# One activation table for logarithm and exponential, and the bids' sigmoid by way of the exponential, in a two-layer kernel on one core

## The chip, the cores and the metric

One core of a Trainium2 chip runs the whole program. The metric is the device time of one execution in microseconds (us): the median of three runs. The engines are named as in the profile: PE (TensorE, with PEld for its weight loads), DVE (VectorE), ACT (ScalarE), POOL (GpSimd) and SP (SyncE, which here issues DMA transfers).

## The reference

Input x is 4 x 2048 tokens of 256 channels, float32. Two layers follow each other; each has an "attention" part and an "ffn" part, with modulated layer norms in front and gated residuals behind. What matters here:

```python
# layer 0, attention: a state-space scan over the tokens
gate = silu(xn @ W_gate)
dt = clip(softplus(z @ W_dt + b_dt), 0.001, 1.0)
h  = exp(dt * A) * h + dt * B * z            # 16 states for each of 512 channels
y  = sum over states of h * C, times gate
# layer 0, ffn: a router's softmax over 8 experts, one expert, exact gelu
probs = softmax(x @ Wr.T);  y = (gelu(x @ W1 + b1) @ W2 + b2) * probs[:, 7]
# layer 1, attention: a second scan, with beta = sigmoid(x @ Wbeta + b_beta)
# layer 1, ffn
conf = sigmoid([h @ conf_rwkv, h @ conf_trans])        # 3 values a token
difficulty = sigmoid(h @ w_diff)                       # 1 value a token
bids = conf * capital_shares * difficulty + h @ W_aff
winner = argmax(bids);  scale = conf[winner] / (conf[winner] + 1e-6)
```

The winner's output (two experts with squared relu, one with a product of two projections) is scaled and added.

## The kernel before

The tokens are cut into 16 chunks of 512 (4 for each batch row). Every engine's program is written out as one list, by chunks. Its backbone is `S_STEPS`, 98 steps a chunk: 23 marks, then 68 units (16 states x 4 blocks of 128 channels, and four steps more for what trails), then the tail. Unit k of a chunk is: ACT fills PSUM bank A0 or A1 in turn with the decay exp(dt * a) (line 1288), DVE runs the scan over the 512 tokens from it and from the input `bu` that POOL has made (lines 1527 and 1100), PE turns the scanned block so that tokens lie on the partitions (line 1760), and DVE multiplies it with C and adds it into `acc` (line 1491). `bu` has 4 buffers; `bb`, the row of B spread over the partitions, has 2, each filled by a DMA for one state (line 930).

Beside the backbone run other streams: `n_stream` prepares a chunk's scan, `f_stream` is layer 0's ffn, `x_stream` is layer 1, `w_stream` the weights' preparation at the start. `weave` puts the pieces of each stream between the steps by due steps in the table `PACE`, one number for each piece and engine. Layer 1 of a chunk falls so into the scan stages of the two chunks after it. Each engine does its list strictly in order; waits are on semaphores, so a wait holds up all that stands behind it on that engine. The last chunk's pieces have due steps of their own (`last_`, `end_`).

The pieces that the change touches, in ACT's order within a chunk: `dt0..3` (Exp of the bias-added product, line 1250), `gate0..3` (Silu, 1256), `ct`, `z0..3`, `softplus0` (Ln of dt + 1, line 1273, due step 10), `softplus1` (16), `lexp` (the router's Exp, line 1329, due 119, which is step 21 of the chunk after), `softplus2` and `3` (21); the units from step 23 on; Tanh pieces `r0`, `r1` (line 1409, due 230 and 231, so steps 34 and 35 two chunks on) and `sW0`, `sW1` (line 1413); `gelu0`, `gelu1` (line 1342); `sg`, the sigmoid of the four values of the bids (line 1428, due 246, step 50). `sg` works on 4 values for each of 4 tokens a partition, 16 elements.

ACT evaluates its functions from a table. A load of a table (`ACT_TABLE_LOAD` in the profile) is placed by the builder ahead of an activation whose function the last loaded table doesn't hold; the kernel before names none itself.

On DVE the piece `choice` (lines 1690 to 1710) waits for `sg`, then makes the bids, the winner and the coefficients in 14 small steps. Each step is followed by a wait for its own semaphore (`own_step`), and `OWN["dve_x"]` states how many such signals `x_stream` gives in a chunk. POOL multiplies `z` by `dt` and then by the first state's row of B (lines 1141 and 1147) as soon as the softplus of a block is there.

Of the kernel before, what the change touches and what calls it, by code (L numbers as in the profile page):

```python
# [8 lines left out]
ALU = mybir.AluOpType  # L9
ACT = mybir.ActivationFunctionType  # L10
# [35 lines left out]

SLOTS = ["ffn_0", "ffn_1", "rv", "sw", "e0_0", "e0_1", "e1_0", "e1_1"]
NSLOT = len(SLOTS)
CREDIT = 1
HB = F // 2 // P  # L50
NHB = F // P
# [34 lines left out]
class Bank:  # L86
# [5 lines left out]
    def fills_before(self, chunk, use):  # L92
        if use in self.last:
            return NCH * len(self.uses) + self.last.index(use) + CREDIT
        return chunk * len(self.uses) + self.uses.index(use) + CREDIT

# [63 lines left out]
def since(eng, sig, chunk, k=0):  # L160

    if sig.at(chunk, k) > 0:
        eng.wait_ge(sig.sem, sig.at(chunk, k))
# [95 lines left out]
def build(nc, w, out):  # L259
    ctx = ExitStack()  # L260
    with ctx:
# [22 lines left out]
        def signal(name, n, first=0):  # L284
            return Signal(sem(name), n, first)
# [129 lines left out]

        w_split = nc.dram_tensor("w_split", (NSLOT, P, 2 * KC * HB * P), F32, kind="Internal").ap()
        mods = nc.dram_tensor("mods", (B, len(ROWS) * C), F32, kind="Internal").ap()
# [5 lines left out]
                for name, uses in BANK_USES.items()}  # L423
        bank_of = {use: bank[name] for name in BANK_USES for use in BANK_USES[name]}
        last_bank_of = {use: bank[name] for name in LAST_USES for use in LAST_USES[name]}

        def bank_at(chunk, use):
            return last_bank_of[use] if chunk == NCH - 1 and use in last_bank_of else bank_of[use]
# [8 lines left out]
        def fill(eng, chunk, use):  # L437

            b = bank_at(chunk, use)
            if b.fills_before(chunk, use) > CREDIT:  # L440
                eng.wait_ge(b.free, b.fills_before(chunk, use))
# [13 lines left out]
        def kp(ap):  # L455
            return ap.rearrange("(k p) m -> p k m", p=P)
# [53 lines left out]
        for X, tag, first in ((X_ALL, "", 0), (X_LAST, "_last", NCH - 1)):  # L510
# [19 lines left out]
            X.x_x5 = signal(f"x_x5{tag}", 1, first)  # L530
            X.o_dve = signal(f"o_dve_x{tag}", OWN["dve_x"], first)
        s_w_last = {name: signal(f"s_w_{name}_last", 16, NCH - 1) for name in ("rv", "sw")}


        o_pool_n = signal("o_pool_n", OWN["pool_n"])
        o_dve_f = signal("o_dve_f", OWN["dve_f"])

# [174 lines left out]
        with nc.Block() as block:  # L712

            @block.sync
            def _(sp):
                for semaphore in [x for b in bank.values() for x in (b.full, b.free)]:
                    sp.sem_inc(semaphore, CREDIT)
                for layer in range(2):
# [150 lines left out]
        def lane_of(j):  # L869

            return X_LAST if j == NCH - 1 else X_ALL
# [16 lines left out]
        def hidden_free(eng, j, name, k):  # L888

            if name == "c":  # L890
                if j == 0:
                    eng.wait_ge(v_low, NSLOT)
                elif j >= 2:
# [28 lines left out]
        with nc.Block() as block:  # L922

            @block.sync
            def _(sp):
# [132 lines left out]
                def w_stream(_):  # L1058
                    yield "fold"
                    for dst, src in ((w_s, w["L1_ffn_Ws"]), (w_2, w["L1_ffn_W2"])):  # L1060
                        sp.dma_start(dst[:, :, :], kp(src)).then_inc(u_fold, 16)
                    for n in range(NSLOT + 1):
                        if n < NSLOT:
                            yield f"in{n}"
# [20 lines left out]
            def _(pool):  # L1085
# [110 lines left out]
                def w_stream(_):  # L1196
                    for n in range(NSLOT):
                        yield f"low{n}"
                        pool.wait_ge(v_high, n + 1)
                        pool.tensor_tensor(wsp[n % 2][:, 1], wst[n % 2][:, :, :], wsp[n % 2][:, 0].bitcast(F32),  # L1200
                                           ALU.subtract).then_inc(v_low, 1)
# [4 lines left out]
            def _(act):  # L1206
# [6 lines left out]
                def n_stream(i):  # L1213
# [55 lines left out]
                           .then_inc(b.free, 1)  # L1269
                    for k in range(DB):  # L1270
                        yield f"softplus{k}"
                        act.wait_ge(s_clip.sem, s_clip.at(i, k + 1))
                        act.activation(dt[:, k, :], dt[:, k, :], ACT.Ln, bias=1.0).then_inc(s_dt.sem, 1)  # L1273

# [91 lines left out]
                def x_stream(j):  # L1366
                    X = lane_of(j)
                    yield "e_norm"
                    if j == 0:
                        for k in range(2):  # L1370
                            act.wait_ge(v_store[k], 16 * NSLOT // 2)
                    since(act, X.x_x5, j)
# [52 lines left out]
                    yield "sg"  # L1425
                    used(act, j, "bidsT")

                    act.activation(X.sg[:, :, :], X.bl[:, :, 0:4], ACT.Sigmoid).then_inc(X.x_sg.sem, 1)
                    for name in "op":
                        for k in range(NHB):  # L1430
                            use = f"{name}{k}"
# [7 lines left out]
                def w_stream(_):  # L1439
# [4 lines left out]
                    for n in range(NSLOT):  # L1444
# [10 lines left out]
                        act.activation(wsp[n % 2][:, 0], wst[n % 2][:, :, :], ACT.Copy).then_inc(v_high, 1)  # L1455

                weave(PACE["act"], step, n_stream, f_stream, x_stream, w_stream)

            @block.vector
            def _(dve):  # L1460
# [126 lines left out]
                def x_stream(j):  # L1587
                    X = lane_of(j)
                    own = Own(dve, X.o_dve, j)
                    own_step = own.step  # L1590
# [91 lines left out]
                    for k in range(KC):  # L1682
# [5 lines left out]
                                                 op0=ALU.add, op1=ALU.mult).then_inc(b.free, 1)  # L1688
                    yield "choice"
                    dve.wait_ge(X.x_sg.sem, X.x_sg.at(j, 1))  # L1690
                    own_step(dve.tensor_tensor(X.bid[:, :, :], X.sg[:, :, 0:3], cs_row[:, :].unsqueeze(1)
                                               .to_broadcast([P, NT, 3]), ALU.mult))
                    own_step(dve.tensor_tensor(X.bid[:, :, :], X.bid[:, :, :], X.sg[:, :, 3:4].to_broadcast([P, NT, 3]),
# [44 lines left out]
                def w_stream(_):  # L1738
# [14 lines left out]
                    dve.memset(carrier[:, :], 0.0).then_inc(v_late, 1)  # L1753

                weave(PACE["dve"], step, n_stream, f_stream, x_stream, w_stream)

            @block.tensor
# [260 lines left out]
                weave(PACE["pe"], step, n_stream, f_stream, x_stream, w_stream)  # L2018


OWN = {"pool_n": 5, "dve_f": 8, "dve_x": 51}


# [20 lines left out]
```

## Time and profile before

| | |
|---|---|
| median of 3 runs | 3285.47 us (3280.89 to 3286.68) |
| span of the profiled execution | 3287.9 us |
| busy: PE, DVE, ACT, POOL | 88%, 83%, 64%, 59% |
| instructions | 45422 |

"Busy" is the time in which an engine has an instruction running; waits, branches and DMA issues aren't counted. In the timelines a row is one instruction or a run of like ones (x3); its first number is the start in us from the span's start, its second the time from the start of the first to the end of the last, and "idle before" names what ended the wait in front of it. Rows of one engine overlap a little, since the end of an instruction and the start of the next do. "issue" as the reason of a wait means that the profile shows nothing that the engine waited for.

### The profile page before, as it was taken

The numbers are of one execution on the slowest core, as the hardware profiler recorded it, in microseconds if no ns is written. First come the engines' busy times: TensorE is split into PE (matmuls) and PEld (weight loads), VectorE is DVE, ScalarE is ACT, GpSimd is POOL, SyncE is SP. The second block draws the span as 40 slices with busy tenths as digits, with TensorE's granted clock in tenths as the row PEclk, the third lists the DMA queues.
The fourth block names the chain that finished last, engine by engine and source line by source line (L and its number), as shares of the span: only waits on it lengthen the run. The fifth ranks groups of instructions, "written<-read, shape, count | busy, mean of one in ns | idle before, by whom it ended". The sixth has DMA issues, their size and how long they took to land.

```text
span 3287.9 us, 45422 instructions
## 1 busy us (share of the span) xinstructions
PE 2907.9 (88%) x14848; PEld 2380.8 (72%) x14848; DVE 2739.3 (83%) x4612; ACT 2096.2 (64%) x3852; POOL 1925.7 (59%) x1541
## 2 busy tenths in 40 slices
PE   6567698998999899898989989899999989998898
PEld 4455477787877778687777868777777877777676
DVE  3777989797998979799898979889897989989541
ACT  2546476676757677675767767576766767575433
POOL 1766667564766757475675756576575647666110
PEclk8558699999999999999999999999999999999998
DMA  4241123231322323232322323232232323223122
GB/s 130 96 159 39 52 81 111 92 102 64 129 82 91 125 78 100 70 118 85 100 103 81 106 79 125 66 106 92 87 109 86 108 76 121 78 71 120 56 103 76
DMA packets 152778, 308.56 MB, mean 94 GB/s; under 512 B 18368, under 2 KB 96984, under 8 KB 135136
## 3 DMA queue, kind: packets, MB, share of 16 engines
q1 hardware_dynamic: 152000, 302.52, 27.6%
q8 instruction: 119, 1.95, 0.2%
q10 hardware_dynamic: 272, 1.57, 0.1%
q0 software_dynamic: 272, 1.57, 0.1%
q14 instruction: 115, 0.94, 0.1%
HBM read 288.27 MB, written 17.35 MB: 93 GB/s over the span
## 4 chain that ended last, share of the span: by engine, by line
PE 48%; DVE 18%; issue 13%; ACT 12%; POOL 5%; DMA 1%; DVEq 0%; SPq 0%; POOLq 0%; ACTq 0%
PE ps_B L1870 11%; PE ps_B L1765 10%; PE ps_A L1765 8%; DVE hs L1527 8%; PE ps_H L1760 7%; DVE acc L1491 5%; PE ps_H L1778 4%; PE ps_B L1760 3%; POOL bu L1100 3%; PE ps_B L1778 3%; PE ps_B L1917 2%; ACT ps_A L1288 2%; DMA bb<-b_rows 1%; DVE hA L1719 1%; ACT acc L1300 1%
## 5 line engine op out<-in xcount | busy, mean ns | idle before, releaser
L1100 POOL TENSOR_TENSOR bu<-z,bb 128x512 f32<-128x512 f32 x1024 | 1294.2, 1290 | 289.9 <-DVE hs L1527 146.7
L1527 DVE TENSOR_TENSOR_SCAN hs<-ps_A,state,bu 128x512 f32<-128x512 f32 x768 | 976.5, 1276 | 21.7 <-ACT ps_A L1288 11.4
L1288 ACT ACTIVATE ps_A<-dt,a_neg 128x512 f32<-128x512 f32 x1024 | 699.3, 686 | 355.7 <-DVE hs L1527 351.5
L1760 PE MATMUL ps_H<-ident,hs 128*128 128x128 f32 x4096 | 652.6, 294 | 195.3 <-DVE acc L1491 123.1
L1760 PEld LDWEIGHTS ps_H<-ident,hs 128*128 128x128 f32 x4096 | 528.3, 151 | 329.2 <-DVE acc L1491 152.0
L1870 PE MATMUL ps_B<-ws_out,hid 128*128 128x256 f32 x2944 | 699.4, 382 | 15.5 <-ACT hid L1437 6.1
L1491 DVE SCALAR_TENSOR_TENSOR acc<-ps_H,ctok,acc 128x512 f32<-128x512 f32 x960 | 700.2, 731 | 8.0 <-PE ps_H L1760 7.1
L1870 PEld LDWEIGHTS ps_B<-ws_out,hid 128*128 128x128 f32 x2944 | 537.0, 191 | 85.1 <-ACT hid L1437 9.9
L1765 PE MATMUL ps_B<-fh,ws_in 128*128 128x512 f32 x1440 | 537.6, 418 | 10.3 <-DVE bl L1680 4.3
L1527 DVE TENSOR_TENSOR_SCAN hs<-ps_A,bu 128x512 f32<-128x512 f32 x256 | 310.9, 1216 | 32.2 <-ACT ps_A L1288 20.0
L1765 PEld LDWEIGHTS ps_B<-fh,ws_in 128*128 128x128 f32 x1440 | 271.0, 188 | 70.5 <-DVE cb L1664 8.1
L1765 PE MATMUL ps_B<-fl,ws_in 128*128 128x512 f32 x720 | 281.9, 391 | 0.0
L1435 ACT ACTIVATE hid<-ps_B 128x512 f32<-128x512 f32 x256 | 149.9, 586 | 174.0 <-PE ps_B L1765 173.4
L1765 PE MATMUL ps_B<-f1h,ws_in 128*128 128x512 f32 x512 | 180.4, 409 | 58.7 <-ACT hid L1334 24.1
L1141 POOL TENSOR_TENSOR z<-z,dt 128x512 f32<-128x512 f32 x64 | 87.0, 1360 | 161.6 <-ACT dt L1273 161.0
L1765 PEld LDWEIGHTS ps_B<-f1h,ws_in 128*128 128x128 f32 x512 | 96.7, 189 | 98.2 <-ACT hid L1334 36.9
L1437 ACT ACTIVATE hid<-hid 128x512 f32<-128x512 f32 x256 | 161.6, 631 | 8.1
L1091 POOL TENSOR_TENSOR rs_f<-rs_f,mhalf 128x4 f32<-128x4 f32 x16 | 16.3, 1017 | 251.9 <-DVE rs_f L1471 251.9
L1595 DVE TENSOR_TENSOR fl<-ff,fh 128x512 fp32r<-128x512 f32 x60 | 46.3, 792 | 134.3 <-ACT fh L1364 134.3
L1765 PEld LDWEIGHTS ps_B<-fl,ws_in 128*128 128x128 f32 x720 | 136.5, 190 | 19.1
L1091 POOL TENSOR_TENSOR rs_x<-rs_x,mhalf 128x4 f32<-128x4 f32 x45 | 49.6, 1103 | 160.9 <-DVE rs_x L1471 160.9
L1778 PE MATMUL ps_H<-w_out,yT 128*128 128x256 f32 x512 | 118.3, 385 | 3.7 <-issue 1.2
(349 smaller groups left out, 4807.7 us busy)
## 6 DMA issues: line engine op xcount, KB each, us to landing
ws_in<-w_split SPq DMA_DIRECT2D x126, 1024.0 KB, 5.4
bb<-b_rows SPq DMA_DIRECT2D x256, 256.0 KB, 3.9
ws_out<-in_L_ffn_V_rwkv SPq DMA_DIRECT2D x64, 512.0 KB, 5.8
ws_out<-in_L_ffn_W SPq DMA_DIRECT2D x32, 512.0 KB, 6.9
xb<-in_L_attn_x SPq DMA_DIRECT2D x16, 512.0 KB, 5.3
n<-in_L_attn_x SPq DMA_DIRECT2D x16, 512.0 KB, 3.9
w_split<-wsp SPq DMA_DIRECT2D x8, 1024.0 KB, 5.6
out<-xb SPq DMA_DIRECT2D x16, 512.0 KB, 3.2
```

The source lines that it names most:

```text
L1091: pool.tensor_tensor(rs[:, :], rs[:, :], mhalf[:, :], ALU.pow).then_inc(own_sig.sem, 1)
L1100: pool.tensor_tensor(bu[:, u % 4, :], z[:, d, :], bb[:, s % 2, :], ALU.mult)\
L1141: pool.tensor_tensor(z[:, k, :], z[:, k, :], dt[:, k, :], ALU.mult).then_inc(s_u.sem, 1)
L1288: act.activation(b.t[:, :], dt[:, d, :], ACT.Exp, scale=a_neg[:, d, s:s + 1])\
L1435: act.activation(hid[:, k, :], b.t[:, :], ACT.Relu).then_inc(b.free, 1)
L1437: act.activation(hid[:, k, :], hid[:, k, :], ACT.Square).then_inc(X.x_sq.sem, 1)
L1491: dve.scalar_tensor_tensor(out=acc[:, t, :], in0=b.t[:, :], scalar=ctok[:, t, s:s + 1], in1=acc[:, t, :], op0=ALU.mult, op1=ALU.add).then_ ...
L1527: dve.tensor_tensor_scan(hs[:, s % 2, d, :], b.t[:, :], bu[:, k % 4, :], state[:, s, d:d + 1] if i % CPB else 0.0, ALU.mult, ALU.add)\
L1760: return pe.transpose(dst, src, ident[:, :])
L1765: last = pe.matmul(dst, a, b, start=n == 0, stop=n == len(prods) - 1)
L1778: last = pe.matmul(b.t[:, t % 2 * C:(t % 2 + 1) * C], act[:, k, t * P:(t + 1) * P], wt[:, k, :], start=k == 0, stop=k == kb - 1)
L1870: last = pe.matmul(b.t[:, t % 2 * C:(t % 2 + 1) * C], hid[:, k, t * P:(t + 1) * P], wt[:, k % HB, :], start=k == 0 and t % 2 == 0, stop=k ...
```

## The change

It is made of two parts. Ahead of the first softplus of each chunk (`softplus0`) a table load is written by hand, with the number of the table that holds both the logarithm and the exponential (`EXP_LN`). And the sigmoid of the bids becomes exp(-x) on ACT in the same place, with two steps on DVE at the head of `choice`: plus one, then the reciprocal, in place in `sg`. `OWN["dve_x"]` goes from 51 to 53.

```diff
@@ -46,6 +46,8 @@
 
 SLOTS = ["ffn_0", "ffn_1", "rv", "sw", "e0_0", "e0_1", "e1_0", "e1_1"]
 NSLOT = len(SLOTS)
+
+EXP_LN = 6
 CREDIT = 1
 HB = F // 2 // P
 NHB = F // P
@@ -424,6 +426,10 @@
         bank_of = {use: bank[name] for name in BANK_USES for use in BANK_USES[name]}
         last_bank_of = {use: bank[name] for name in LAST_USES for use in LAST_USES[name]}
 
+        def table_of_exp_and_ln(act):
+            act.add_instruction(mybir.InstLoadActFuncSet(name=nc.get_next_instruction_name(), engine=act.engine,
+                                                         act_func_set_id=EXP_LN))
+
         def bank_at(chunk, use):
             return last_bank_of[use] if chunk == NCH - 1 and use in last_bank_of else bank_of[use]
 
@@ -1269,6 +1275,8 @@
                            .then_inc(b.free, 1)
                     for k in range(DB):
                         yield f"softplus{k}"
+                        if k == 0:
+                            table_of_exp_and_ln(act)
                         act.wait_ge(s_clip.sem, s_clip.at(i, k + 1))
                         act.activation(dt[:, k, :], dt[:, k, :], ACT.Ln, bias=1.0).then_inc(s_dt.sem, 1)
 
@@ -1425,7 +1433,7 @@
                     yield "sg"
                     used(act, j, "bidsT")
 
-                    act.activation(X.sg[:, :, :], X.bl[:, :, 0:4], ACT.Sigmoid).then_inc(X.x_sg.sem, 1)
+                    act.activation(X.sg[:, :, :], X.bl[:, :, 0:4], ACT.Exp, scale=-1.0).then_inc(X.x_sg.sem, 1)
                     for name in "op":
                         for k in range(NHB):
                             use = f"{name}{k}"
@@ -1688,6 +1696,8 @@
                                                  op0=ALU.add, op1=ALU.mult).then_inc(b.free, 1)
                     yield "choice"
                     dve.wait_ge(X.x_sg.sem, X.x_sg.at(j, 1))
+                    own_step(dve.tensor_scalar(X.sg[:, :, :], X.sg[:, :, :], 1.0, None, ALU.add))
+                    own_step(dve.reciprocal(X.sg[:, :, :], X.sg[:, :, :]))
                     own_step(dve.tensor_tensor(X.bid[:, :, :], X.sg[:, :, 0:3], cs_row[:, :].unsqueeze(1)
                                                .to_broadcast([P, NT, 3]), ALU.mult))
                     own_step(dve.tensor_tensor(X.bid[:, :, :], X.bid[:, :, :], X.sg[:, :, 3:4].to_broadcast([P, NT, 3]),
@@ -2018,7 +2028,7 @@
                 weave(PACE["pe"], step, n_stream, f_stream, x_stream, w_stream)
 
 
-OWN = {"pool_n": 5, "dve_f": 8, "dve_x": 51}
+OWN = {"pool_n": 5, "dve_f": 8, "dve_x": 53}
 
 
 # ---- launch: one core; inputs and outputs as the reference has them ----
```

## Rows read from the trace of the kernel before

**Rows 1.** The page: span, and busy time of each engine
```profile
span 3287.9 us, 45422 instructions
...
PE 2907.9 (88%) x14848; PEld 2380.8 (72%) x14848; DVE 2739.3 (83%) x4612; ACT 2096.2 (64%) x3852; POOL 1925.7 (59%) x1541
```

**Rows 2.** Window, chunk 6: from:to, length, busy us of PE, PEld, DVE, ACT, POOL
```profile
1257.60:1326.40 68.80, 66.86 (x366) 56.69 (x364) 68.44 (x82) 48.99 (x102) 53.88 (x46) 1.00 0.34 113
```

**Rows 3.** Timeline of ACT, chunk 6, from the softplus to the scans
```profile
1192.56 1.28 ACT L1273 ACT_TABLE_LOAD   x1
...
1198.90 1.28 ACT L1329 ACT_TABLE_LOAD   x1
1200.19 0.23 ACT L1329 ACTIVATE lg<-lg 128x32 f32<-128x32 f32 x1
```

**Rows 4.** Timeline of DVE, chunk 6, the same stretch
```profile
1198.35 0.84 DVE L1563 TENSOR_TENSOR lg<-lg,lg_m 128x32 f32<-128x32 f32 x1
...
1201.67 0.68 DVE L1595 TENSOR_TENSOR fl<-ff,fh 128x512 fp32r<-128x512 f32 x1
1202.27 3.62 DVE L1527 TENSOR_TENSOR_SCAN hs<-ps_A,state,bu 128x512 f32<-128x512 f32 x3
1206.15 6.26 DVE L1527 TENSOR_TENSOR_SCAN hs<-ps_A,state,bu 128x512 f32<-128x512 f32 x5 [0.26 <-POOL bu L1100]
1212.63 1.28 DVE L1527 TENSOR_TENSOR_SCAN hs<-ps_A,state,bu 128x512 f32<-128x512 f32 x1 [0.21 <-issue]
```

**Rows 5.** Timeline of POOL, chunk 6, the same stretch
```profile
1194.62 1.28 POOL L1141 TENSOR_TENSOR z<-z,dt 128x512 f32<-128x512 f32 x1 [8.06 <-ACT dt L1273]
...
1201.80 1.70 POOL L1100 TENSOR_TENSOR bu<-z,bb 128x512 f32<-128x512 f32 x1
...
1204.83 11.24 POOL L1100 TENSOR_TENSOR bu<-z,bb 128x512 f32<-128x512 f32 x9
```

**Rows 6.** Waits: who waited for what, us in total, times, longest
```profile
DVE hs L1527 <- POOL bu L1100: 13.0, 25, 1.6
```

**Rows 7.** Groups of ACT's instructions: busy us and mean ns, idle before
```profile
L1288 ACT ACT_TABLE_LOAD x30 | 38.5, 1283 | 0.6
...
L1329 ACT ACT_TABLE_LOAD x15 | 19.2, 1283 | 0.3
L1428 ACT ACT_TABLE_LOAD x15 | 19.2, 1283 | 0.3
```

**Rows 8.** Timeline of ACT, chunk 6, around the first Tanh
```profile
1214.87 0.59 ACT L1409 ACTIVATE cb<-ps_B 128x512 f32<-128x512 f32 x1
1215.78 0.69 ACT L1288 ACTIVATE ps_A<-dt,a_neg 128x512 f32<-128x512 f32 x1 [0.32 <-DVE hs L1527]
...
1218.72 0.60 ACT L1409 ACTIVATE cb<-ps_B 128x512 f32<-128x512 f32 x1 [1.64 <-PE ps_B L1765]
```

**Rows 9.** Timeline of PE, chunk 6, start of the second product (r1)
```profile
1217.05 0.48 PE L1765 MATMUL ps_B<-fh,ws_in 128*128 128x512 f32 x1
```

**Rows 10.** Timeline of DVE, chunk 6, the scan that takes that decay
```profile
1218.73 1.27 DVE L1527 TENSOR_TENSOR_SCAN hs<-ps_A,state,bu 128x512 f32<-128x512 f32 x1
```

**Rows 11.** Timeline of ACT, chunk 6, around the sigmoid
```profile
1250.89 1.28 ACT L1428 ACT_TABLE_LOAD   x1
...
1260.12 0.60 ACT L1435 ACTIVATE hid<-ps_B 128x512 f32<-128x512 f32 x1 [5.71 <-PE ps_B L1765]
```

**Rows 12.** Timeline of DVE, chunk 6, inside the choice
```profile
1254.82 0.17 DVE L1691 TENSOR_TENSOR bid<-sg,cs_row 128x12 f32<-128x12 f32 x1
...
1257.05 0.18 DVE L1707 RECIPROCAL wcs<-wcs 128x4 f32<-128x4 f32 x1
1257.26 0.16 DVE L1708 TENSOR_TENSOR wcs<-wcs,bmax 128x4 f32<-128x4 f32 x1
```

**Rows 13.** Timeline of DVE, tail of the run, behind the last choice
```profile
3227.64 0.88 DVE L1719 SCALAR_TENSOR_TENSOR hA_last<-ps_A,coef_last,hA_last 128x256 f32<-128x256 f32 x2 [1.28 <-PE ps_A L1778]
```

**Rows 14.** Timeline of DVE, chunk 5, second scan behind the choice
```profile
1073.08 1.28 DVE L1527 TENSOR_TENSOR_SCAN hs<-ps_A,state,bu 128x512 f32<-128x512 f32 x1 [0.51 <-issue]
```

## The prediction

> **What bounds the kernel now.** The page comes first [rows 1]: one core, span 3287.9 us, PE busy 88%, DVE 83%, ACT 64%. No engine is idle enough to be ignored, and none is full, so the shares decide nothing; the kernel has 16 chunks of about 189 us and has to be read by stage. I took chunk 6 (1192 to 1391 us) and checked its readings in the others.
>
> Second, the windows: in the scan stage DVE is busy 68.44 of 68.80 us [rows 2]. That stage is 64 scans and their read-outs in a fixed order, and DVE has no gap in it: a microsecond added to DVE there is added to the chunk, unless DVE next waits for something that did not move.
>
> Third, the start of the scan stage, on three engines. ACT loads a table at 1192.56, runs the first softplus, and after the last softplus loads another table at 1198.90 for the router's exponential [rows 3]. DVE starts scans 0 to 2 at 1202.27, then waits 0.26 us for POOL; scans 3 to 7 start 1.25 us apart; scan 8 waits 0.21 us more [rows 4]. POOL makes the scan inputs `bu`: it starts at 1194.62, when the first softplus is there, and from then on has no gap: `z`, `bu`, `z`, `bu`, ..., then nine `bu` in 11.24 us, 1.25 us each [rows 5]. Scan 3 starts 0.04 us after its `bu` ends (1204.83 + 1.25 = 1206.08, to within the rounding of merged rows). So the scan stage is started by POOL, POOL by the first softplus, and the second table load is not in that line. Over the run DVE's scans wait 13.0 us for `bu`, in 25 places [rows 6]; chunks 2 to 15 all have the wait before scan 3, 0.25 to 0.46 us long, and chunks 0 and 1 a longer one.
>
> **The change, part by part.** All prices are from one profiled execution (span 3287.9); the median of the runs is 3285.47, 2.4 us less and inside the runs' own spread of 5.8, so I work out a difference and add it to the median.
>
> *The load before the first softplus.* It takes the place of the one at 1192.56 [rows 3], one in each of 16 chunks. Same time, same place: 0.
>
> *The load before the router's exponential* (15 times 1.28 us [rows 7]) goes; in chunk 0, where the softplus is followed by the first decay, one of line 1288's 30 goes. The exponential needs DVE's subtraction, which ends at 1198.35 + 0.84 = 1199.19 [rows 4], so it can start at about 1199.24 instead of 1200.19 [rows 3]: 0.95 us earlier, not 1.28. Behind it come DVE's `prob`, one split, and scans 0 to 2, all 0.95 earlier. Scan 3 isn't: it waits for POOL, and what is late next is `bu`, every time until scan 7. Cover: POOL's queue. Worth 0 here. Bounds: if DVE and POOL get in each other's way differently (POOL's `bu` at 1201.80 took 1.70 instead of 1.27 while DVE's split ran [rows 4, 5]) scans 3 to 7 may move by 0.43 either way; the split still falls on one POOL instruction, the one before, so I take 0. Scan 8's 0.21 has no releaser in the trace; it may go since PE and ACT are ahead: between 0 and 15 x 0.21 = 3.2 us gained. I take 0, as the row calls it issue.
>
> *A table for Tanh.* Today the table loaded for the exponential at 1198.90 also serves the Tanh at 1214.87, for no load stands between. No row shows whether the new common table holds Tanh. If not, a load comes 14 times before line 1409 (chunks 2 to 15; the first two have no Tanh there), after which the decays' Exp needs none, as now. ACT's load then costs between 0 and 1.28 us. I take that it comes. What it delays: the Tanh from 1214.87 to 1216.15, and behind it in ACT's queue the decay at 1215.78, to about 1216.75 to 1217.4. ACT's next Tanh waits for PE until 1218.72, with 1.64 us idle before it [rows 8]. The decay is for the scan at 1218.73 [rows 10] (the scans take turns on two banks), 1.3 us later. PE's product `r1`, which starts at 1217.05 [rows 9], needs the bank that the Tanh frees, at 1216.75 instead of 1215.46: 0.3 us in hand. Cost 0; if the weight load ahead of `r1` wants the bank earlier, up to 14 x 0.2 = 2.8 us; if nothing covered it, 14 x 1.28 = 18 us.
>
> The Trainium skill, "ScalarE: Activation LUTs", section "Table sets: the hidden batching unit", names tanh among the functions in exp's set and only exp and ln for the common set. By that the load does come, as taken here; no row of this kernel shows it.
>
> *The bids' sigmoid.* Sigmoid's load (15) goes, and the Exp load behind it (line 1288; 14 of the 30 are this one, the others are those after Gelu and chunk 0's) [rows 7]. The last Sigmoid but one, in the tail, keeps a load, since Gelu's came before it. That is 2.57 us less on ACT in chunks 2 to 15, in chunk 6 from 1250.89 on. What waits for it? One decay, whose scan comes only behind DVE's choice, and after that ACT is idle 5.71 us for PE [rows 11]. DVE itself came for the sigmoid at 1254.82 [rows 12]. So 0: ACT idles longer. The new Exp activation costs what the Sigmoid did.
>
> In all ACT has 30 loads fewer (2 in each of 14 chunks, 1 in chunks 0 and 1): 30 x 1.28 = 38.5 us less of its 2096.2 [rows 1], none of it on the path by the above.
>
> The same page's section "What ACT_TABLE_LOAD costs" puts a switch at about 2.66 us, 1283 ns of load and 1380 of drain. By that ACT would be spared 80 us. Here the instruction starts 0.01 us behind the load (1198.90 + 1.28, 1200.19 [rows 3]), so the trace bears out the load and not the drain.
>
> *Plus one and reciprocal on DVE.* The 14 steps that are there, each waited for before the next, start 0.20 us apart in the mean (1254.82 to 1257.05 for eleven), the reciprocal 0.21 [rows 12]. The new two work on 16 elements a partition instead of 4: 2 x 0.21 = 0.42 us a chunk. They can't start early: DVE gets to them when it has done the two `tw` products. They lie before scan 26, in the stage without gaps. Choices 0 to 13 lie there: 14 x 0.42 = 5.9 us. Choice 14 and 15 lie in the tail; behind the last, DVE waits 1.28 us for PE [rows 13], so they cost 0.
> What takes some of it back: two scans later, in some chunks, DVE waits for `bu`, since POOL waits for a row of `b` whose transfer is queued behind weights. In chunk 5 this is 0.51 us [rows 14]; I find such waits in six of the 14 chunks, 0.2 to 0.7 us long (0.26, 0.51, 0.28, 0.69, 0.20, 0.42), which take back 0.26 + 0.42 + 0.28 + 0.42 + 0.20 + 0.42 = 2.0 us. In chunk 6 the `bu` is there 0.5 us early and nothing is taken back.
>
> **Sum.** 5.9 - 2.0 = +3.9 us: 3291.8 in the profile's terms, 3289.4 as median. Own range: with scan 8's gap gained 0.7; with nothing taken back and `r1` late 5.9 + 2.8 = 8.7. About 3286 to 3294.
>
> **Rivals.**
> 1. The start of the scan stage does follow ACT: the 0.95 us passes through, because POOL too gains from DVE being out of its way earlier. 15 x 0.95 = 14.3 us gained, 5.9 lost: 3277.1. For it: ACT has no gap between softplus, load and exponential [rows 3], and DVE is behind it. Against: `bu` ends just before each of scans 3 to 7.
> 2. Slower: the Tanh load is on the path. It decides if PE's `r1` or the decay behind it has less in hand than 1.28 us; by the rows they have 1.6 and 2.3. Price up to 14 x 1.28 = 18: 3285.5 + 3.9 + 17.9 = 3307.3.
> 3. The hand-written load isn't counted by what places the others: then the softplus has two loads, 1.28 us on the line softplus, POOL, scan in 16 chunks, and the exponential's loads stay: 3285.5 + 20.5 + 3.9 = 3309.9.
>
> The skill's rule in the same page, "Rules for kernel authors", to group by table set and to use the common set for exp and ln, would have the time fall, as rival 1 does. The trace agrees that the loads fall away, and not that anybody waits for them.
>
> **How the numbers follow.** Forecast 0.70, rival 1 0.12, rival 2 0.12, rival 3 0.06. The forecast is the likeliest: 3289.4. The medians themselves are uncertain by some 3 us (the runs spread over 5.8), so the forecast's range becomes 3282 to 3296. For 8 in 10 part of the rivals, which may come in at a fraction, is taken in: 3279 to 3298. A change under 0.2% (6.6 us) can't be told from none here. Faster than 3278.9 is rival 1 at nearly full price, 0.12; slower than 3292.0 is rivals 2 and 3 and the upper end of the forecast's own range, 0.25; between them 0.63.
>
> **What would show it.** Right: 80 loads instead of 110; scan 3 still 0.03 us behind its `bu` and 12.3 us behind the first softplus, with its wait grown from 0.26 to about 1.2 us; 16 steps at the choice, 0.42 us more; the wait of chunk 5 down from 0.51 to 0.1; ACT's idle time up by what it is spared. Wrong: scan 3 earlier after the softplus (rival 1); PE idle before `r1` for ACT, or scans waiting for a decay (rival 2); two loads in a row before the softplus (rival 3). What would also make it wrong is a new order of DVE and POOL on their shared work, 0.4 us a time, which the trace of before can't tell.

## The result: 3294.03 us, and the profile of the changed kernel

| | before | changed |
|---|---|---|
| median of 16 runs each | 3285.66 (3280.89 to 3287.78) | 3294.03 (3284.95 to 3299.27) |
| span of the profiled execution | 3287.88 | 3297.48 |
| ratio of the times, 95% interval | | 1.0018 (1.0010 to 1.0026) |

By the ratio, 0.18%, that is under the prediction's bound of 0.2% and on the slow side of none. By the medians it is over it: they are 8.4 us apart, 0.26%, and 3294.03 lies above the prediction's 3292.0, in the stretch to which it gave 0.25. The median is 4.6 us above the forecast and inside the range. The two measures part where times lie in two groups, as the changed kernel's do: six of 16 at 3285.0 to 3287.4, ten at 3293.8 to 3299.3; the profile is of the upper one. In one other kernel such a gap lies in TensorE's clock in the tail, as is shown further down; no profile caught the lower group of this one.

The page of the changed kernel (its parts are those of [rows 1]), then the groups of ACT's table loads ([rows 7]) and the wait of DVE's scans for POOL ([rows 6]):

```profile
span 3297.5 us, 45424 instructions
...
PE 2920.5 (89%) x14848; PEld 2379.6 (72%) x14848; DVE 2745.5 (83%) x4644; ACT 2059.5 (62%) x3822; POOL 1929.1 (59%) x1541
```

```profile
L430 ACT ACT_TABLE_LOAD x16 | 20.5, 1283 | 0.3
...
L1296 ACT ACT_TABLE_LOAD x15 | 19.2, 1283 | 0.3
L1417 ACT ACT_TABLE_LOAD x14 | 18.0, 1283 | 0.2
```

```profile
DVE hs L1535 <- POOL bu L1106: 48.3, 40, 16.9
```

ACT has 30 instructions and 36.7 us fewer: the loads are 80 instead of 110 (with 16 each for Silu and Gelu, one in the tail and two at the start). L430 is the load by hand, L1296 the decays' after Gelu, L1417 the one that comes ahead of Tanh. DVE has 32 instructions more. And DVE waits 48.3 us for `bu`, where it waited 13.0: 16.9 us of it is one wait in the first chunk that the profile of before put down to ACT (17.6), and the other 18.4 us more are new, 14 times 1.26 in chunks 2 to 15 and 0.7 in chunk 0: what ACT gave up at the router stands again as DVE's wait for POOL.

The start of the scan stage in chunk 6, timelines of ACT, DVE and POOL, to be laid beside [rows 3 to 5]:

```profile
1192.96 1.28 ACT L430 ACT_TABLE_LOAD   x1
1194.26 0.63 ACT L1281 ACTIVATE dt<-dt 128x512 f32<-128x512 f32 x1
...
1199.62 0.23 ACT L1337 ACTIVATE lg<-lg 128x32 f32<-128x32 f32 x1 [0.32 <-DVE lg L1571]
```

```profile
1200.84 0.68 DVE L1603 TENSOR_TENSOR fl<-ff,fh 128x512 fp32r<-128x512 f32 x1
1201.44 2.45 DVE L1535 TENSOR_TENSOR_SCAN hs<-ps_A,state,bu 128x512 f32<-128x512 f32 x2
1204.08 1.28 DVE L1535 TENSOR_TENSOR_SCAN hs<-ps_A,state,bu 128x512 f32<-128x512 f32 x1 [0.19 <-POOL bu L1106]
1206.69 6.26 DVE L1535 TENSOR_TENSOR_SCAN hs<-ps_A,state,bu 128x512 f32<-128x512 f32 x5 [1.33 <-POOL bu L1106]
1213.16 1.28 DVE L1535 TENSOR_TENSOR_SCAN hs<-ps_A,state,bu 128x512 f32<-128x512 f32 x1 [0.21 <-issue]
```

```profile
1195.03 1.28 POOL L1147 TENSOR_TENSOR z<-z,dt 128x512 f32<-128x512 f32 x1 [8.09 <-ACT dt L1281]
...
1200.86 1.82 POOL L1147 TENSOR_TENSOR z<-z,dt 128x512 f32<-128x512 f32 x1
...
1205.38 9.97 POOL L1106 TENSOR_TENSOR bu<-z,bb 128x512 f32<-128x512 f32 x8
```

From the first softplus (1194.26) to scan 0 it is 7.18 us instead of 8.42, but to scan 3 it is 12.43 instead of 12.30. All of chunks 2 to 15 show it (12.41 to 12.45, before 12.28 to 12.32); chunks 0 and 1 are within 0.03 us of what they were. POOL's eight products up to that scan's take 11.60 us instead of 11.46. The row to see is POOL's `z` at 1200.86: 1.82 us, where this instruction otherwise takes 1.28. DVE's `prob`, its split `fl` and the first scan ran beside it. Before, DVE's split and scan fell on the `bu` at 1201.80 and stretched it to 1.70 [rows 5].

The choice in the same chunk, timeline of DVE:

```profile
1255.35 0.17 DVE L1699 TENSOR_SCALAR sg<-sg 128x16 f32<-128x16 f32 x1
1255.55 0.25 DVE L1700 RECIPROCAL sg<-sg 128x16 f32<-128x16 f32 x1
1255.83 0.17 DVE L1701 TENSOR_TENSOR bid<-sg,cs_row 128x12 f32<-128x12 f32 x1
```

The two new steps take 0.20 and 0.28 us, 0.48 together, from start to start.

To find where the rest lies I cut the run at the starts of certain rows (first softplus, scans 3, 8, 26, 28 and 63 of a chunk) and added each stretch up over chunks 2 to 15, all from one profile per kernel. "Front" is from a chunk's last scan to the next chunk's first softplus (13 of them), "start" what lies before chunk 2's first softplus, "tail" from the last scan of all. Last column: us of the middle (chunks 2 to 15) in which PE was granted 1.2 GHz, not 2.4. In us:

| kernel | start | softplus to scan 3 | scans 3 to 8 | 8 to 26 (choice) | 26 to 28 | 28 to 63 | fronts | tail | span | at 1.2 GHz |
|---|---|---|---|---|---|---|---|---|---|---|
| before | 437.0 | 172.2 | 90.5 | 629.2 | 76.1 | 1027.1 | 608.2 | 247.7 | 3287.9 | 115.5 |
| changed | 436.4 | 174.1 | 90.4 | 635.7 | 73.7 | 1027.8 | 608.3 | 251.0 | 3297.5 | 122.8 |
| changed, third profile | 433.6 | 174.1 | 90.4 | 635.5 | 73.2 | 1027.7 | 606.4 | 249.7 | 3290.5 | 117.3 |
| table alone | 433.1 | 174.1 | 90.4 | 629.4 | 75.1 | 1027.1 | 606.6 | 250.7 | 3286.5 | 116.2 |
| sigmoid alone | 436.6 | 172.2 | 90.5 | 635.6 | 73.1 | 1028.8 | 608.1 | 250.1 | 3295.0 | 120.5 |
| two more steps | 436.4 | 174.1 | 90.7 | 641.9 | 73.0 | 1028.5 | 609.5 | 250.7 | 3304.9 | 130.0 |
| router's load back | 435.5 | 172.2 | 90.8 | 635.5 | 73.2 | 1028.1 | 607.3 | 247.4 | 3289.9 | 119.3 |
| another load, then Tanh's | 434.4 | 174.2 | 90.4 | 645.9 | 73.2 | 1027.7 | 610.4 | 250.3 | 3306.5 | 126.8 |

The scan stages (the five columns in the middle) went from 1995.0 to 2001.8 us, +6.8; in the third profile of the changed kernel it is +5.8. That part is the steadier one from profile to profile. Start, fronts and tail together are not steady: +2.8 in the first profile, -3.2 in the third. The tail alone is 2.0 to 3.3 us longer in both: the clock record has PE at 1.2 GHz for 13.7 us from some 30 us behind the last scan on, where it is 10.2 us in the kernel before.

### The profile page after: what moved, and what is told of

It reads as the page before. It is cut to its first block, busy times and chain, and to the rows that moved or that the text cites. A ratio compares the mean times of both kernels' runs of the same rounds, so it can differ in the third digit from the quotient of the medians.

```text
span 3297.5 us, 45424 instructions
## 1 busy us (share of the span) xinstructions
PE 2920.5 (89%) x14848; PEld 2379.6 (72%) x14848; DVE 2745.5 (83%) x4644; ACT 2059.5 (62%) x3822; POOL 1929.1 (59%) x1541
## 4 chain that ended last, share of the span: by engine, by line
PE 47%; DVE 17%; issue 13%; ACT 10%; POOL 7%; DMA 3%; SPq 0%; DVEq 0%; POOLq 0%; ACTq 0%
PE ps_B L1775 10%; PE ps_B L1880 10%; DVE hs L1535 8%; PE ps_A L1775 8%; PE ps_H L1770 7%; DVE acc L1499 5%; POOL bu L1106 4%; PE ps_H L1788 4%; DMA bb<-b_rows 3%; PE ps_B L1770 3%; PE ps_B L1927 2%; PE ps_B L1788 2%; POOL z L1147 2%; DVE hA L1729 1%; ACT ps_A L1296 1%
## 5 line engine op out<-in xcount | busy, mean ns | idle before, releaser
L1296 ACT ACTIVATE ps_A<-dt,a_neg 128x512 f32<-128x512 f32 x1024 | 699.2, 686 | 381.7 <-DVE hs L1535 377.8
L1880 PEld LDWEIGHTS ps_B<-ws_out,hid 128*128 128x128 f32 x2944 | 536.2, 191 | 90.8 <-issue 14.1
L1147 POOL TENSOR_TENSOR z<-z,dt 128x512 f32<-128x512 f32 x64 | 94.8, 1482 | 160.9 <-ACT dt L1281 160.1
L1603 DVE TENSOR_TENSOR fl<-ff,fh 128x512 fp32r<-128x512 f32 x60 | 46.2, 790 | 136.6 <-ACT fh L1372 136.6
```

What stands on the lines that cost most here:

```text
L1147: pool.tensor_tensor(z[:, k, :], z[:, k, :], dt[:, k, :], ALU.mult).then_inc(s_u.sem, 1)
L1296: act.activation(b.t[:, :], dt[:, d, :], ACT.Exp, scale=a_neg[:, d, s:s + 1])\
L1880: last = pe.matmul(b.t[:, t % 2 * C:(t % 2 + 1) * C], hid[:, k, t * P:(t + 1) * P], wt[:, k % HB, :], start=k == 0 and t % 2 == 0, stop=k ...
```

## The experiments

The edits are shown shortened: slices, semaphore updates, the definitions of the numbers of tables and the count `OWN` are left out.

**One part at a time.** `e1_table_only` keeps the Sigmoid activation and leaves the two DVE steps out; `e2_sigmoid_only` leaves the tables to the builder.

```diff
 e1, against the changed kernel
-  act.activation(X.sg, X.bl[:, :, 0:4], ACT.Exp, scale=-1.0)
+  act.activation(X.sg, X.bl[:, :, 0:4], ACT.Sigmoid)
-  own_step(dve.tensor_scalar(X.sg, X.sg, 1.0, None, ALU.add))
-  own_step(dve.reciprocal(X.sg, X.sg))
 e2, against the changed kernel
-  if k == 0:
-      table_of_exp_and_ln(act)
```

> The hand-written table load ahead of softplus0 alone; the bids keep their Sigmoid and DVE its 14 steps. Theory (the time is lost at DVE's two new steps, 0.48 us in each of 14 chunks, and the loads are hidden): the router's load is gone as in the changed kernel, and scans 3 to 7 start 12.43 us after softplus0 instead of 12.29, since POOL's z product at 1200.86 is stretched by DVE's split to 1.82 us: +0.14 us in 14 chunks, 2 us in all; s8 to s26 as before. Median about 2 us over the kernel before. Rival (the Tanh load or the new table is what costs): it carries the whole loss, 6 to 8 us. Rival 1 of the prediction (a removed load at the start is on the path): 10 us or more faster.

> The bids' sigmoid as Exp on ACT plus two steps on DVE; no table load by hand, so softplus keeps its own and the router's Exp its load; Sigmoid's load and the one behind it go. Theory: choice 0.48 us longer in 14 chunks, 6.7 us, of which about 2 are taken back where DVE waited for bu two scans later: 4 to 5 us over the kernel before; scan 3 at 12.29 us after softplus0 as before. Rival (the table costs): within 1 us of the kernel before.

Measured: the table alone 3288.3 us against 3286.51 of before (ratio 1.0003, 0.9995 to 1.0012), the sigmoid alone 3292.93 (1.0015, 1.0006 to 1.0023). In the table above the two effects stand apart, each in its own column: 14 x 0.14 = 2.0 us from softplus to scan 3 with the table alone, 14 x 0.46 = 6.4 at the choice with the sigmoid alone, 2.9 of it taken back two scans later. In the scan stages 1.2 and 5.3 make 6.5, against 6.8 for both; the medians' 1.8 and 6.4 make 8.2, against 8.3 for the changed kernel on the same chip. So the hand-loaded table, which takes away the 15 loads ahead of the router's exponential, gains nothing. By the stages it costs 1 to 2 us; the times alone do not show that, since their interval holds 1.

**The choice has no cover.** `e4_two_more_steps` adds two steps of the same size, and `after_again` is the changed kernel once more, on the same chip.

```diff
   own_step(dve.reciprocal(X.sg, X.sg))
+  own_step(dve.tensor_scalar(X.sg, X.sg, 1.0, None, ALU.mult))
+  own_step(dve.tensor_scalar(X.sg, X.sg, 1.0, None, ALU.mult))
```

> The changed kernel with two further steps (times one, on 16 elements a partition) behind the reciprocal: the suspected cost doubled. Theory: each step starts 0.20 us after the one before, 0.40 us a chunk, 5.7 us over the changed kernel less what waits for bu are left to take back (under 0.5): about 5 us over it, 11 over the kernel before. Rival (DVE has slack at the choice): 0.

> The changed kernel once more, for a second profile. Its 16 runs fell into two groups, 3285 to 3287 and 3294 to 3299 us, at a mean granted clock of 0.941 to 0.943 and 0.937 to 0.940. Theory: what differs between the groups is how long PE's clock stays at the lower level where PE has been idle, in the chunks' fronts and above all in the tail (247.7 us from the last scan in the kernel before, 251.0 in the changed kernel's profile, with nothing else changed there); DVE's stages are equal to 0.1 us a chunk. Rival: the groups differ in the scan stage (waits for bu).

Measured: 3305.53 us (ratio 1.0053, 1.0038 to 1.0068), 10.7 above the 3294.85 of the changed kernel beside it, where about 5 were expected. The stage with the choice grew by 6.2 (14 x 0.44), and nothing more was taken back, so the mechanism holds and the sum doesn't. Against the profile of `after_again` (span 3294.2; choice 635.9, start 433.8, fronts 608.1, tail 250.3, 120.2 us at 1.2 GHz) the span is 10.7 longer: 6.1 at the choice, 2.6 at the start, 1.4 in the fronts, 0.4 each in the tail and from scan 3 to 8. The steps themselves are the 6.1. The 1.4 in the fronts go with 3.6 us more at 1.2 GHz there. The 2.6 at the start do not go with the clock (239 us at 1.2 GHz there, against 242); that column differs by as much between profiles of the changed kernel itself, and why is left open.

**The router's load back.** `e5_router_load_back` puts a load by hand ahead of the router's exponential.

```diff
+  table_of_exp_and_ln(act)
   act.activation(lg, lg, ACT.Exp)      # lexp
```

> The changed kernel with a table load of 1.28 us put back ahead of the router's Exp. Theory (a load there is hidden behind POOL, and without it DVE's split falls on POOL's z product, 1.82 us, instead of on bu, 1.70): scans 0 to 2 start later again, but scan 3 comes 12.29 instead of 12.43 us after softplus0, 2 us over 14 chunks, so this kernel is about 2 us faster than the changed one although it does more. Rival (the load's removal is worth something): 5 us or more slower.

Timelines of ACT, DVE and POOL of this kernel, chunk 6:

```profile
1199.08 1.28 ACT L430 ACT_TABLE_LOAD   x1 [0.32 <-DVE lg L1572]
1200.38 0.23 ACT L1338 ACTIVATE lg<-lg 128x32 f32<-128x32 f32 x1
```

```profile
1202.14 3.62 DVE L1536 TENSOR_TENSOR_SCAN hs<-ps_A,state,bu 128x512 f32<-128x512 f32 x3
1206.03 6.29 DVE L1536 TENSOR_TENSOR_SCAN hs<-ps_A,state,bu 128x512 f32<-128x512 f32 x5 [0.27 <-POOL bu L1106]
```

```profile
1200.32 1.27 POOL L1147 TENSOR_TENSOR z<-z,dt 128x512 f32<-128x512 f32 x1
1201.68 1.70 POOL L1106 TENSOR_TENSOR bu<-z,bb 128x512 f32<-128x512 f32 x1
```

The load is there, 1.28 us on ACT in each chunk, and the stretch from softplus to scan 3 is *shorter* by 1.9 us over the run (172.2, as before): DVE comes later, POOL's `z` stays at 1.27, and the next `bu` takes 1.70. The wait of scan 3 is back to 0.27. The median was 3293.78, the changed kernel's own; its ten executions (3290.6 to 3297.2) cannot show 1.9 us.

**The bids' two loads back.** `e6_bid_loads_back` puts a load by hand ahead of the bids' Exp and one behind it.

```diff
+  table(act, EXP_ONLY)
   act.activation(X.sg, X.bl[:, :, 0:4], ACT.Exp, scale=-1.0)
+  table(act, EXP_ONLY)
```

> The changed kernel with two table loads put back around the bids' Exp, 2.57 us of ACT a chunk. Theory (ACT idles 5.7 us behind them): all stages as in the changed kernel, to 1 us over 14 chunks. Rival (the freed ACT time is used by somebody): 5 us or more slower.

Timeline of ACT, chunk 6:

```profile
1250.46 1.28 ACT L434 ACT_TABLE_LOAD   x1 [1.02 <-DVE bl L1694]
1251.76 0.22 ACT L1441 ACTIVATE sg<-bl 128x16 f32<-128x16 f32 x1
1251.99 1.28 ACT L434 ACT_TABLE_LOAD   x1
...
1258.69 0.60 ACT L1449 ACTIVATE hid<-ps_B 128x512 f32<-128x512 f32 x1 [4.72 <-PE ps_B L1781]
```

3294.9 us, and the five columns of the scan stages are within 0.7 us of the changed kernel's. The 32 loads cost nothing here: ACT still idles 4.72 us for PE behind them.

**What is in hand ahead of Tanh.** The forecast had 1.6 us in hand for the Tanh load. A first try, `e3_two_tanh_loads`, wrote a twin load there.

```diff
+  table(act, EXP_ONLY)      # e3
+  table(act, EXP_ONLY)
   act.activation(X.cb[:, k, :], b.t[:, :], ACT.Tanh, scale=0.5)     # r0
```

> The changed kernel with one more table load of 1.28 us ahead of the first Tanh (two instead of one) in 14 chunks. Theory: the first load is covered, with about 0.2 us in hand before PE's product r1 (bank free at 1217.41, r1 at 1217.59 in the changed kernel's chunk 6), so the second isn't: r1 starts about 1.1 us later and DVE's second cb step waits for it, 0.5 to 1.1 us a chunk, 7 to 15 us in all over the changed kernel, in the stage from scan 8 to scan 26. If ACT has a slack of more than 2.6 us there: that stage is as in the changed kernel, 635.7 us over 14 chunks.

```profile
L434 ACT ACT_TABLE_LOAD x14 | 18.0, 1283 | 0.2
```

The group of loads has 14 at that line, not 28. Of the two loads of one table a single one remains, so this was the changed kernel again (3294.63 us), and it says nothing of the slack. The second try loads another table first.

```diff
+  table(act, SIGMOID)       # e10
+  table(act, EXP_ONLY)
```

> The changed kernel with a load of another table (Sigmoid's) and then of Tanh's, both ahead of the first Tanh of the stage, so that the Tanh comes another 1.28 us later in 14 chunks. The twin loads of one table tried for this before did not both remain in the trace. The forecast had 0.3 us in hand at PE's product r1 behind the first load, and rows of the changed kernel show r1 0.54 us later than before in chunk 6 with no scan late. Theory (ACT's and PE's queues have slack there of over two loads against the scans): 94 loads instead of 80, r1 up to 1.28 us later, the sums of the scan stage unchanged, time within 3 us of the changed kernel (3291 to 3298). Rival (a load there is paid for once its slack is used up): scan 8 to 26 of each chunk up to 14 x 0.9 to 1.28 = 13 to 18 us longer, with scans waiting for a decay: 3306 to 3313.

Timelines of ACT, PE and DVE, chunk 6, behind the two loads; then ACT and PE of the changed kernel at the same place:

```profile
1217.29 2.57 ACT L435 ACT_TABLE_LOAD   x2
1219.87 0.60 ACT L1425 ACTIVATE cb<-ps_B 128x512 f32<-128x512 f32 x1
```

```profile
1220.52 0.50 PE L1783 MATMUL ps_B<-fh,ws_in 128*128 128x512 f32 x1 [0.91 <-ACT cb L1425]
```

```profile
1223.57 0.69 DVE L1680 SCALAR_TENSOR_TENSOR cb<-cb,ps_B 128x512 f32<-128x512 f32 x1 [0.47 <-PE ps_B L1783]
```

```profile
1215.52 1.28 ACT L1417 ACT_TABLE_LOAD   x1
1216.81 0.60 ACT L1417 ACTIVATE cb<-ps_B 128x512 f32<-128x512 f32 x1
...
1219.27 0.60 ACT L1417 ACTIVATE cb<-ps_B 128x512 f32<-128x512 f32 x1 [0.67 <-PE ps_B L1775]
```

```profile
1217.59 0.48 PE L1775 MATMUL ps_B<-fh,ws_in 128*128 128x512 f32 x1
```

The theory of much slack falls, and the rival holds. With one load PE's `r1` starts without a wait; with two it waits 0.91 us, DVE's product behind it 0.47, and the stage grows by 10.2 us, 0.73 a chunk. The time was 3309.07 (ratio 1.0068, 1.0053 to 1.0083), 15.7 above the changed kernel's 3293.36 on the same chip. Between the two profiles the span differs by 16.0: 10.4 in this stage, 4.0 in the fronts, 1.4 at start and tail. So of the second 1.28 us 0.55 were hidden: the first load fits with about half a microsecond to spare.

**Where ACT's line begins.** By the chain softplus, POOL, scan, time is to be gained ahead of the first softplus. `e8_load_early_sigmoid` is the kernel before with the common table loaded ahead of `z1`, in an idle 0.69 us of ACT. `e9_softplus_early` does that and runs softplus 0 and 1 ahead of `z2` and `z3` (due steps 6 instead of 10 and 16). `e11_softplus_early_no_table` is that order without the hand-loaded table.

```diff
 e9, against the kernel before
-  for k in range(DB): z{k}
-  for k in range(DB): softplus{k}
+  z0, table_of_exp_and_ln, z1, softplus0, softplus1, z2, z3, softplus2, softplus3
 e8: the load alone, in the same place; e11: the same order, no load
```

> The hand-written table alone (the bids keep their Sigmoid, DVE has no new steps), its load moved ahead of z1, where ACT waits for PE, and the first two softplus moved ahead of z2. If POOL's queue, started by the first softplus, sets the start of the scans, this must move it: POOL starts z and bu some 3 to 4 us earlier, and scan 3 then follows DVE's own work (scans 0 to 2 without a wait), about 1.5 us a chunk earlier than in the changed kernel: 20 us faster than it, 12 to 20 us faster than the kernel before. Rival (ACT's or PE's own work sets the start): within 5 us of the kernel before.

> The kernel before with the common table loaded by hand ahead of z1, where ACT is idle 0.69 us for PE, instead of right ahead of the first softplus; the bids' Sigmoid and the order of the steps kept. Theory (the line softplus, POOL, scan carries what ACT saves ahead of the softplus): the softplus comes 0.6 to 0.7 us earlier, 14 x 0.65 = 9 us gained, less the 2 us that the common table alone cost: 3278 to 3282. Rival (the start of the stage hangs on something else): 3287 to 3289.

> The kernel before with nothing but the order changed: softplus 0 and 1 ahead of z2 and z3; the tables are left to the builder, so the router's exponential has its load again. The same kernel with the common table took 3261.3. Theory (the load ahead of the router's exponential is worth nothing as long as POOL's queue covers it, and something as soon as it doesn't): with the softplus early POOL has its first four products done by 1182.8 and scan 3 waits only 0.24 us for bu, so the load's 1.28 us less 0.24 comes onto the path: first softplus to scan 3 some 14 x 1.0 = 14 us longer than with the common table, 3272 to 3278. Rival 1 (the common table is worth nothing here too, all of the 26 us are the order's): 3260 to 3264. Rival 2 (the order is worth nothing, the earlier place of the load was all of it): 3284 to 3287.

| kernel | median us | ratio, 95% | start | softplus to scan 3 | fronts | tail | span | at 1.2 GHz |
|---|---|---|---|---|---|---|---|---|
| e8 | 3283.0 | 0.9985 (0.9976 to 0.9995) | 429.1 | 184.2 | 598.5 | 241.0 | 3273.7 | 119.2 |
| e9 | 3261.32 | 0.9920 (0.9906 to 0.9935) | 425.6 | 211.5 | 553.0 | 247.7 | 3260.2 | 95.1 |
| e11 | 3307.45 | 1.0065 (1.0050 to 1.0080) | 426.8 | 242.4 | 566.2 | 250.1 | 3305.3 | 137.2 |

`e9` beats both kernels: it is 0.8%, 26 us, below the kernel before. Its span is 27.7 us shorter: 55.2 are gained in the fronts, of which 39.3 are given back from softplus to scan 3, and 11.4 are gained at the start. `e8` gained 9.7 us in the fronts, as expected, and gave 12.0 back from softplus to scan 3. The row that says why is POOL's second `z`, idle for a softplus that stands in ACT's queue behind a piece that waits for PE:

```profile
1189.86 1.28 POOL L1147 TENSOR_TENSOR z<-z,dt 128x512 f32<-128x512 f32 x1 [1.11 <-ACT dt L1281]
```

An earlier softplus 0 without an earlier softplus 1 is worth nothing in the middle of the run. What `e8` has left, 4.0 us between the medians (3278 to 3282 was expected, 3283.0 came), can be from the start, 8.0 us less in the profile, where profiles of the changed kernel differ by 2.9. The tail's 6.7 us less are those of the quickest of its executions, which is the one profiled, and not of the median.

`e11` missed what each theory had said. Timelines of ACT, DVE and PE, chunk 6, and a window over PE's 14 matrix products and transposes behind the norm (columns as in [rows 2]; the third number from the end is the granted clock):

```profile
1186.47 1.28 ACT L1274 ACT_TABLE_LOAD   x1
...
1199.07 1.28 ACT L1330 ACT_TABLE_LOAD   x1
```

```profile
1200.63 0.19 DVE L1568 TENSOR_REDUCE lg_m<-lg 128x4 f32<-128x32 f32 x1 [1.86 <-ACT lg L1330]
```

```profile
1190.94 1.97 PE L1761 MATMUL ps_B<-ident,nn 128*128 128x128 f32 x8 [2.40 <-ACT nn L1209]
```

```profile
1190.94:1195.06 4.12, 4.03 (x14) 3.26 (x14) 0.00 (x0) 1.09 (x2) 2.90 (x3) 0.60 0.00 0
```

The same in `e9`:

```profile
1174.80 1.28 ACT L430 ACT_TABLE_LOAD   x1
```

```profile
1186.57 0.19 DVE L1576 TENSOR_REDUCE lg_m<-lg 128x4 f32<-128x32 f32 x1 [0.44 <-ACT lg L1338]
```

```profile
1179.84 1.09 PE L1769 MATMUL ps_B<-ident,nn 128*128 128x128 f32 x8 [1.36 <-ACT nn L1215]
```

```profile
1179.84:1182.42 2.58, 2.49 (x14) 1.88 (x14) 0.00 (x0) 1.09 (x2) 2.50 (x3) 1.00 0.00 0
```

The spans of `e11` and `e9` differ by 45.1 us, nearly all of it three things. First, the fronts, 13.3 longer. The builder's load stands behind `z1`, right ahead of the softplus, where nothing hides it: from `z0` to the softplus it is 3.39 us instead of 2.59, 10.3 in 13 fronts. The other 2.9 lie ahead of `z0`; the fronts have 7.5 us more at 1.2 GHz. Second, the router's load is now on the path, since with the softplus early POOL is no longer the last: in five chunks scan 3 comes 1.26 us later after the softplus, nearly the whole load. Third, in the other nine it comes 2.6 to 2.9 later. There PE, which waits 2.4 us for the norm instead of 1.36, does the same 14 instructions in 4.12 us at a mean clock of 0.60 instead of 2.58 at 1.00, and its result is what the router waits for. The second and third make the 31.0 us from softplus to scan 3. (In the five chunks PE's wait was 2.40 us too, and the clock 1.00, so the wait alone doesn't decide the clock.)

So the common table is worth nothing to the order of the kernel before, and with its place ahead of `z1` up to 45 us to another order. No run has the early order with the common table loaded right ahead of the softplus, so table and place are told apart by these rows alone.

**A profile of the lower group.** `after_third` repeats the changed kernel.

> The changed kernel once more, for a profile of one of its quicker executions, since its times lie in two groups, 3284.7 to 3287.4 and 3293.8 to 3299.3. If this profile is of the lower group: the scan stages' sums as in the first profile (choice stage +6.5), and 8 to 10 us less between the last scan of a chunk and the next softplus or in the tail, where PE is at the lower clock less long. If it is of the upper group: as in the first profile, and the question stays open.

It had 3293.36 us (3284.84 to 3295.73), and its profile (3290.5) is again not of the lower group. What such a group is, the profile of `e8` shows by chance: its ten times are 3275.5, 3276.3 and eight from 3281.5 to 3284.8, and the profile is of the quickest. Window of 23.9 us over the tail, from 164 us after the last scan on in `e8` and then from 166 us on in the changed kernel of `after_again`, from where PE's clock falls in each:

```profile
3196.80:3220.70 23.90, 17.26 (x68) 13.03 (x69) 6.79 (x23) 7.92 (x14) 0.00 (x0) 0.79 0.27 104
```

```profile
3210.50:3234.40 23.90, 15.25 (x40) 10.73 (x41) 6.13 (x29) 5.47 (x10) 1.22 (x2) 0.50 0.35 132
```

In every other profile PE has 1.2 GHz for 23.9 us here; in that one it came back to full clock after 10.2 us, ran 68 products in the window instead of 40, and the tail took 241.0 us instead of 247.4 to 251.0. `e5`, with the same clock in the rest of its tail, has 247.4, so the stretch is worth 6.4 us; `e8`'s two quickest times lie 5 to 9 us below the others. That the changed kernel's lower group, 6 to 14 us below the upper, is the same is argued from this, not shown.

## Why the prediction was right, and where a term was off

The time is inside the stated range, and the path that the prediction told for each part is the one that the runs show. Its bound of 3292.0 for "slower" was passed, with 0.25 given to that.

*The load before the softplus, 0:* right. L430 has 16 rows of 1.28 us in the place of the old ones.

*The router's load, worth 0:* right that it isn't gained, with the mechanism as told: scan 0 comes 1.24 us sooner (forecast 0.95; `prob` is shorter too, 0.61 us where it was 0.86) and DVE waits 1.33 us before scan 3 (forecast about 1.2) and 0.19 before scan 2. The term was mis-sized by 2 us: it is +0.14 a chunk, not 0. The bound of 0.43 for "DVE and POOL get in each other's way differently" held it. I took 0, on the ground that the split would still fall on one POOL instruction. That ground was too weak: it does, but the instruction stretched is now `z`, with 1.82, instead of `bu`, with 1.70, and `e5` shows both cases with nothing else changed. Scan 8's gap of 0.21 stayed, as taken.

*The table for Tanh:* right. Fourteen loads at L1417. The Trainium skill, "ScalarE: Activation LUTs", section "Table sets: the hidden batching unit", names tanh beside exp, and for the common set only ln and exp, with the rest of its list left open; the 14 rows agree that a load comes. That the load costs nothing was right, but narrow: 0.3 us in hand at `r1` by the forecast, and `e10` shows that another 1.28 us costs 0.73 a chunk. Rival 2 was wrong about this load and right about the next.

*The sigmoid's loads, 0:* right, by `e6`. The drain of about 1380 ns that the Trainium skill, "ScalarE: Activation LUTs", section "What ACT_TABLE_LOAD costs", adds to a load is not seen: the softplus starts 0.02 us behind the load (1192.96 + 1.28, 1194.26), and ahead of all 16 loads of L430 ACT idles 0.3 us together.

*The two steps, 0.42 a chunk:* right place, a little small. They take 0.48: the reciprocal of 16 elements a partition runs 0.25 us (mean 253 ns of 15) and not 0.18 like that of 4. I had priced both by the pitch of steps on 4 to 12 elements. In the stage it comes to 6.5 us, 14 times 0.47, instead of 5.9.

*Taken back, 2.0:* 2.3 in the profile (26 to 28), 2.9 with the sigmoid alone. The wait of 0.51 in chunk 5 [rows 14] is gone altogether, not down to 0.1.

The sum for the scan stages was +3.9 and is +6.8 (5.8 in the third profile). By terms: +1.9 for the start of the stage, +0.6 for the steps, -0.3 for what is taken back, and +0.7 elsewhere in the scan stages, mostly from scan 28 to 63, whose cause is left open. The other 1.7 of the median's 4.6 us, and +2.8 of the profile, are start, fronts and tail, which the forecast did not carry as a term. The 1.7 is inside the 3 us that the prediction left to the medians; between the first and the third profile of the changed kernel these parts shrank by 6.0 (start 2.9, fronts 1.9, tail 1.3), and each of them has less time at 1.2 GHz in the third (242.3, 22.7 and 44.9 us against 249.2, 25.6 and 46.2).

*Rival 1*, that the stage's start follows ACT, is refuted by `e1` and `e5`; *rival 3*, two loads ahead of the softplus, by the count of L430. (Rival 1's price of 3277.1 leaves out the 2.0 us taken back; with them it is 3275.1. Nothing hangs on it.) The warning at the end, a new order of DVE and POOL, is what came.

## What to carry to other kernels

Before you price a removed stall, find the engine that is last at the next meeting point: here ACT gave up 36.7 us, and DVE waited for POOL instead. Then turn the question round: what would have to move so that the saving is on the path? Once two softplus steps ran earlier, the same table and its hand-picked place divided 3261 us from 3307. And count the instances of what an experiment inserted before reading its time: one of these was the unchanged program.

## What the runs showed of the hardware

Some elementwise instructions of POOL and DVE stretch where they meet, and most do not. POOL's 128x512 product goes from 1.28 us to between 1.66 and 1.82 only where it starts beside DVE's split `fl`: 27 products in the profile of before and 27 in that of the changed kernel, out of 28 such meetings in each (the other one takes 1.38). A split that starts when a product is well under way takes 1.15 us instead of 0.68 itself, and leaves that product at 1.28. Beside scans alone POOL's products keep 1.28 in the mean of some 950. DVE's subtraction of 128x32 takes 0.84 beside POOL's `z` [rows 4] and 0.19 in `e9` and `e11`, where POOL is idle until it ends or nearly so. Which of POOL's instructions is hit is worth 0.14 us here.

The granted clock differs between stretches with the same work, and between executions of one program. Windows over two fronts of the changed kernel, with the same matrix products in them (columns as in [rows 2]):

```profile
1148.27:1194.26 45.99, 45.07 (x234) 36.41 (x232) 34.30 (x96) 24.33 (x42) 14.01 (x10) 0.99 0.20 68
1337.37:1384.55 47.18, 46.10 (x234) 37.01 (x232) 34.53 (x96) 24.33 (x41) 13.99 (x10) 0.97 0.14 42
```

The granted clock is 0.99 in one and 0.97 in the other, and the second takes 1.19 us longer. In the kernel before the lengths (46.0 to 46.8 and 47.1 to 47.5 us) change places nearly chunk by chunk, with six long of 13; in the changed one two long ones follow each other twice, and eight are long. In the sum the fronts are equal here (608.2 and 608.3 us), but 606.4 in the third profile: between kernels that differ by a few microseconds this moves by a good part of the change itself.
